# Down copies and slot pair 0's normalisation ahead of the last shared silu, last down products ahead of pair 0's gate and up

## The reference

```
xn = layernorm(x)
s  = recurrence(xn, W_hg) @ W_out          # per channel: h = (1 - sigmoid(gate)) * h + sigmoid(gate) * (relu(hidden) + 0.5)
shared = (silu(xn @ Sg) * (xn @ Su)) @ Sd
routed = sum over a token's 2 best of 16 experts: p_e * (silu(xn @ Wg_e) * (xn @ Wu_e)) @ Wd_e
out = x + s * silu(routed + shared)
```

## Time and profile before

| | us |
|---|---|
| median of 3 timed runs | 329.79 |
| lowest and highest | 329.20, 330.83 |
| the profiled execution, whole | 327.45 |
| its span, first to last instruction | 325.7 |

### The profile page before, as it was taken

How to read it: one execution, slowest core, us unless ns; L and a number is a source line. 1 busy time by engine, 2 the same in 40 slices (tenths; PEclk the granted TensorE clock), 3 DMA queues, 4 the chain that set the end, 5 groups by cost and what they waited for, 6 DMA issues and landing times.

```text
span 325.7 us, 5997 instructions
## 1 busy us (share of the span) xinstructions
PE 291.7 (90%) x1523; PEld 198.5 (61%) x1523; DVE 252.0 (77%) x634; ACT 241.4 (74%) x517; POOL 201.2 (62%) x242
## 2 busy tenths in 40 slices
PE   0699999999989999996968999999999999999920
PEld 0357767766656666663645676777777777777620
DVE  7399999999999799999451778787878787878830
ACT  1789999999975777985664777777787878787520
POOL 3997446530137776878667777665656566656670
PEclk9999999999998999998999999999999999999985
DMA  8999999690006885333795435755656454541000
GB/s 233 303 372 393 440 445 399 228 432 3 0 28 204 279 256 215 124 127 147 247 405 195 168 107 194 208 176 149 180 149 181 150 181 129 168 127 51 19 0 0
DMA packets 28256, 63.62 MB, mean 195 GB/s; under 512 B 3717, under 2 KB 22672, under 8 KB 27456
## 3 DMA queue, kind: packets, MB, share of 16 engines
q1 hardware_dynamic: 21184, 45.58, 41.3%
q0 software_dynamic: 6752, 17.06, 14.2%
q10 hardware_dynamic: 288, 0.60, 0.6%
HBM read 29.32 MB, written 35.14 MB: 198 GB/s over the span
## 4 chain that ended last, share of the span: by engine, by line
PE 78%; ACT 5%; issue 5%; POOL 4%; DVE 3%; DMA 1%; POOLq 0%; ACTq 0%; DVEq 0%
PE p_u L998 21%; PE p_u L926 20%; PE p_s L1023 10%; PE p_s L937 8%; PE p_sh L1010 5%; PE p_lg L907 4%; PE p_sh L946 4%; PE p_xt L974 3%; POOL out L354 2%; PE p_xt L894 2%; DMA arena<-in_x 1%; POOL arena L310 1%; ACT arena L457 1%; ACT rec L427 1%; ACT rec L420 1%
## 5 line engine op out<-in xcount | busy, mean ns | idle before, releaser
L354 POOL DMA_INDIRECT out<-arena x83 | 82.1, 989 | 46.4 <-DVE arena L825 30.0
L926 PE MATMUL p_u<-xT,w_front 128*128 128x512 f32 x192 | 93.9, 622 | 3.2 <-DVE prod L569 2.5
L348 POOL DMA_INDIRECT slots<-arena,pos x64 | 71.4, 1116 | 28.7 <-issue 16.1
L998 PE MATMUL p_u<-arena 128*128 x166 | 78.3, 593 | 0.0
L926 PEld LDWEIGHTS p_u<-xT,w_front 128*128 128x128 f32 x192 | 34.9, 198 | 35.4 <-issue 33.9
L1023 PEld LDWEIGHTS p_s<-arena,rec 128*128 128x128 f32 x332 | 43.4, 191 | 21.2 <-issue 21.2
L799 DVE TENSOR_TENSOR rec<-p_u,rec 128x512 f32<-128x512 f32 (+1 forms) x42 | 28.8, 685 | 29.3 <-ACT rec L473 29.3
L480 ACT ACTIVATE rec<-p_sh 128x512 f32<-128x512 f32 (+1 forms) x42 | 24.9, 592 | 30.8 <-PE p_sh L1010 30.8
L1023 PE MATMUL p_s<-arena,rec 128*128 x332 | 44.1, 276 | 1.3 <-ACT rec L480 1.3
L998 PEld LDWEIGHTS p_u<-arena 128*128 128x128 f32 x166 | 28.3, 190 | 19.6 <-issue 19.6
L561 DVE TENSOR_TENSOR_SCAN rec<-rec 128x512 f32<-128x512 f32 x32 | 39.3, 1229 | 1.1
(11 more groups left out here) (130 smaller groups left out, 440.5 us busy)
## 6 DMA issues: line engine op xcount, KB each, us to landing
slots<-arena SPq DMA_DIRECT2D x4, 4116.0 KB, 27.0
arena<-slots SPq DMA_DIRECT2D x41, 392.0 KB, 3.3
arena<-in_W_lines SPq DMA_DIRECT2D x2, 2304.0 KB, 11.3
arena<-in_x SPq DMA_DIRECT2D x16, 256.0 KB, 5.3
arena<-in_W_lines SPq DMA_DIRECT2D x4, 768.0 KB, 4.5
out<-arena POOLq DMA_INDIRECT x83, 2.7
slots<-arena,pos POOLq DMA_INDIRECT x64
w_front<-in_W_front ACTq DMA_DIRECT2D x1, 392.0 KB, 3.6
```

The source lines that it names most:

```text
L348: pool.indirect_dma_start(slots, index, xrow[:, t], None).then_inc(s_disp[t % WINDOW], 16)
L354: pool.indirect_dma_start(out, index, xg[:, n % RX, h, X], None, bounds_check=T - 1, oob_is_err=False)\
L926: nc.tensor.matmul(p_u[:, n % 4], w_front[:, UPS[q]:UPS[q] + P], xT[:, c % XB], start=True, stop=True)\
L998: last = nc.tensor.matmul(p_u[:, n % 2 * 2 + h], xsT[:, n % 2, h * P:(h + 1) * P], w_lines[:, bass.DynSlice(line_at[2 * n + h], 4 * P)], s ...
```

## The change

In ScalarE's stream, in the last chunk (i = 15), `copy_down(14)` and `normalise_slots(0)` are moved ahead of `shared_silu(15)`. Behind the chunk loop the order becomes: copy of transpose 0, normalise 1, normalise 2, `copy_down(15)`, copy of transpose 1, and the slot loop, whose step 0 no longer holds normalise 2. In TensorE's stream the order becomes: offsets 0, transpose 0, `rec_down(15)`, `shared_down(15)`, transpose 1, gate and up of pair 0, offsets 1. No instruction is added or left out, no buffer and no semaphore changes, and the streams of VectorE, GpSimd and SyncE are untouched.

```diff
                 for c in read(i)[-1:]:
                     copy_xT(c)
+                if i == NCH - 1:
+                    copy_down(i - 1)
+                    normalise_slots(0)
                 shared_silu(i)
-                if i >= 1:
+                if 1 <= i < NCH - 1:
                     copy_down(i - 1)
...
-            for n in range(2):
+            copy_slot_xT(0)
+            for n in range(1, 3):
                 normalise_slots(n)
-                copy_slot_xT(n)
             copy_down(NCH - 1)
+            copy_slot_xT(1)
             for n in range(PAIRS):
                 if 1 <= n < PAIRS - 1:
                     copy_slot_xT(n + 1)
                 if n >= 3:
                     ffn_gate(n - 3)
-                if n + 2 < PAIRS:
+                if 3 <= n + 2 < PAIRS:
                     normalise_slots(n + 2)
                 block_silu(n)
...
-            def first_slots():
-                slot_transpose(0)
-                load_keys(0)
-                slot_transpose(1)
-                gate_up(0)
-                load_keys(1)
-
...
-            first_slots()
+            load_keys(0)
+            slot_transpose(0)
             rec_down(NCH - 1)
             shared_down(NCH - 1)
+            slot_transpose(1)
+            gate_up(0)
+            load_keys(1)
             for n in range(1, PAIRS):
```

## The result

Twenty timed runs of each order on the chip of the result:

| us | before | after |
|---|---|---|
| median | 329.31 | 328.96 |
| lowest, highest | 324.52, 331.17 | 326.68, 331.99 |
| runs under 328 | 8 of 20 | 5 of 20 |
| profiled execution, whole | 327.45 | 330.90 |
| its span | 325.7 | 329.2 |

What follows compares the result with a forecast made beforehand. TensorE was taken to bound the slot stage, waiting on ScalarE's normalise at the passage. Saving 4.7 us there, less 1.29 and 0.20 for the loads of pairs 10 and 11, left 3.2: 329.79 - 3.2 = 326.6 us, range 324.4 to 328.4.

Steps and rivals of the forecast that it cites:

- The passage: TensorE from the last up products of chunk 15 to transpose 3: three waits on normalise go, saving 4.7 us.
- silu 15: ScalarE in the last chunk: silu 15 starts at 166.76, 0.49 us later than before, at no cost.
- VectorE's product behind it: After silu 15: VectorE's product ends near 168.1, before `shared_down(15)` asks for it at 169.1.
- hidden transposes 0: TensorE after gate and up of pair 1: one new wait of 0.10 us for VectorE's rows of pair 0.
- The load of pair 10: Slot stage: this load follows the 64th dispatch and pair 0's stores, lands at 197.90, and leaves 3.40 us of the gain.
- Nothing of this moves: GpSimd's dispatches, first store at 190.18 and pair 10's load keep their times, since GpSimd waits for neither engine between dispatches.
- the wait of 1.29 us: TensorE ahead of transpose 10: it arrives at 197.55 but can't start before 198.84, because of pair 10's load.
- My bounds of the cap: Landings of the loads of pairs 10 and 11, taking 3.2 or 4.0 us: 3.2 or 2.4 us of saving left.
- The third rival: Loads of pairs 10 to 16 land 3 us later and eat the saving: 329.6 us, chance 0.06.
- the second rival: TensorE's clock falls at the new wait for pair 10's load, costing 1.6 us: 328.0 us, chance 0.15.
- waits of that length at the passage left the clock alone: Argument against a clock fall at pair 10: waits of 1.57 and 1.62 us had left the clock at 1.00.
- the first rival: Full 4.7 saving (325.1 us), or a passage clock fall in before's timed runs that the change removes (325.0); chance 0.30.

Runs made afterwards that it cites:

- b_again: The kernel before, unaltered, run again on chip 3: median 342.80 us, ratio to before 1.0036.
- b_short2: The kernel before with the last 8 of 64 dispatches left out, on chip 4: median 335.38 us, ratio to before 0.9758.
- b_short3: The kernel before with the last 8 of 64 dispatches left out, on chip 3: median 337.12 us, ratio to before 0.9820.
- a_short: The changed kernel with the last 8 of 64 dispatches left out, on chip 2: median 338.3 us, beside 363.0 for before.
- a_short2: The changed kernel with the last 8 of 64 dispatches left out, on chip 4: median 331.55 us, ratio to before 0.9685.
- a_short3: The changed kernel with the last 8 of 64 dispatches left out, on chip 3: median 331.41 us, ratio to before 0.9635.
- a_again3: The changed kernel, unaltered, on chip 9: median 343.16 us, ratio to before 0.9985.
- a_again2: The changed kernel, unaltered, run again on chip 2: median 361.0 us, ratio to before 0.996.
- a_rx12_3: The changed kernel with twelve buffers for slot pairs instead of ten, on chip 3: median 341.95 us, ratio to before 0.9937.
- b_late3: The kernel before with six memsets on GpSimd ahead of its last 24 dispatches, on chip 9: median 349.87 us, ratio to before 1.0138.

## Why the prediction was wrong

**The passage: right, to 0.1 us.** Forecast 4.7, measured 4.75 in the profile. No wait at transpose 0; silu 15 at 167.51, where the forecast 166.76 plus the 0.83 by which this profile runs later gives 167.59; VectorE's product behind it over at 168.8, ahead of `shared_down(15)` at 169.77; hidden transposes 0 with a new wait of 0.27 (forecast 0.10).

**The load of pair 10: the right mechanism, the wrong size.** The step that failed reads "Nothing of this moves", with GpSimd's first store at 190.18 and the landing at 197.90, taken from the one profile of before. The moved instructions don't move it, but it differs between the two profiles. In the profile of after the 64th dispatch came 4.9 us later, the load landed at 202.25, and the wait of 1.29 us became 4.72. My bounds of the cap, 2.4 to 3.2 us left, were made from how long a load takes (3.2 and 4.0 us), and left out when it is issued, which came 5.2 us later here (199.11 against 193.90). The third rival, loads landing 3 us later and 329.6 us, names what the profile of after shows; it was given 0.06, because the landings of the earlier trace rows differ by only 0.8, and both of them are from one execution. With these dispatches the old order would have waited too: its transpose 10, due at 202.24 + 0.83 = 203.07, could not start before 202.25 + 0.94 = 203.19. Both orders come to transpose 10 at the same time, which is argued from the rows; no run of the old order on that chip with late dispatches was profiled.

**The clock behind the wait: the second rival, mis-sized.** It was given 0.15 and 1.6 us. The wait was longer, the lower level held for both gate and up and into the down product, and cost 2.5 us. Of the twenty timed runs of the new order, twelve have a mean granted clock of 0.966 or 0.967, as the profiled one does, and take 329.7 us on average; the other eight have 0.970 to 0.976 (the profile of before has 0.974) and take 327.9. That is what a fall in some runs and not in others would look like, though only one of them was profiled. The sentence against this rival, "waits of that length at the passage left the clock alone", rested on the one profile in which they did; in b_again, b_short2 and b_short3 pair 0's gate and up behind the waits of the passage take 2.83, 3.62 and 3.03 us, not 1.96. So the second half of the first rival, a fall at the passage in runs of before which the new order takes away, is shown on chips 3 and 4 (the profiles of a_short, a_short2, a_short3, a_again3 and after have none there). On the chip of the result the one profile of before has none, and how often its other runs do isn't known. The Trainium skill's rule ("TensorE: Matmul & The Clock Gate", "HAM oscillation") is that waits for DMA between groups of matmuls throw the array back to the lower clock. The trace of after agrees, with 0.50 from 203 us behind the wait for the load. The 0.50 rows at 152 us in before and at 176 in b_short2 stand behind waits for VectorE and for ScalarE's normalise, which that section doesn't speak of.

**Sum.** By the profiles, the new order reaches the end at transpose 10 plus 123.5 us, plus 2.5 where the clock falls, and transpose 10 is the later of TensorE's own time and about 9.4 to 10 us after the 64th dispatch. With the dispatches of the profile of before that is 198.84 + 123.5 = 322.3 of span, 324.1 us whole (whole less span is 1.75), and 326.6 with the fall; with the dispatches of the profile of after it is 330.9. The twenty runs lie from 326.7 to 332.0, and none comes near 324.1. The old order, with its waits, with or without a fall of 1.4 to 2.8 at the passage and with either profile's dispatches, comes out between 327.5 and 331, which leaves out its six quickest runs, 324.5 to 327.3. That the two medians meet is argued from these sums, not shown run by run. Shown is that the saving exists (from the last up products to transpose 3 the new order takes 9.42 to 13.2 us in eleven of its twelve profiles, the old one 14.17 or more in all eight of its own; only a_again2, held up on chip 2, takes 18.9). Shown is also that it is kept where 8 dispatches are left out (chips 4 and 3), and that the profile of after loses 4.9 and 2.5 us behind it. The wait of several us at pair 10 is in that one profile only: no other run had TensorE there before its load, so none tested it.

One reading of the prediction is off, and nothing hangs on it: of the stores' idle time in the earlier trace rows, 30.0 of 46.4 us end on VectorE, two thirds and not half.

**What stays open**: why the 41st dispatch comes when it does, and why later in the new order's profiles; how often either order waits at pair 10 on the chip of the result; what the quickest runs of before do; what makes ScalarE stand on the other chips; what a filled wait does. Of the versions with all their work done, only a_rx12_3 lies below before by more than its interval, by 0.6%, and on chips 4 and 9 twelve buffers don't repeat it.

## What to carry to other kernels

An engine that is busy for nearly all of a stage and shows no wait can still be a few us from another bound (3.4 here, from 198.84 to 202.24): list, for each thing that it will ask for earlier, when that thing is there and what its time hangs on, down to the first instruction of the other engine's queue. Take the spread of that moment from more than one execution, since one profile gives one draw; here two profiles differ by 4.9 us, more than the saving. A wait moved from one place to another isn't only its own length: the clock that it brings down behind it is part of its price at both places.

## What the runs showed of the hardware

- Two waits of about 1.5 us with a transpose pair between left TensorE's clock at 1.00 in the first profile of the old order and brought it to 0.50 in b_short2 and b_short3, for 2.8 and 1.4 us, and in b_again, where the first of them was 2.27 us long. A wait of 4.72 us cost 2.5 more behind it.
- The last of GpSimd's 64 indirect dispatches starts 4.9 us later in the profile of after than in that of before, and all of it is there at the 41st, ahead of anything that the change moves. The unaltered new order has it at 193.84 us in one profile and at 189.72 in another, on another chip.
- Chips differ. The same kernel takes 329 us on one, 343 to 346 on three others (3, 4 and 9) and 363 on a fifth (2), where two sets of runs gave 363.0 and 363.7. On chips 3, 4 and 9 part of the loss is in the chunk stage, whose last up products start 0.5 to 8 us later than on the first chip (20 in b_late3). The larger part in the kernels with all dispatches lies at 177 to 197 us, where ScalarE stands idle for up to 5.9 us ahead of instructions whose products are over. With the last 8 of 64 indirect dispatches left out, chip 3 takes 337.1 us instead of 343.5 in the old order, and 331.4 in the new, where the new order with twelve buffers and all dispatches takes 342.0.
